# Attention stage of a GNN kernel: ACT and PE read the gathered rows in place, and a gather unit is signalled later

## What is computed

```python
h = (x @ W_att).reshape(n, H, D)
e = a_src[src] + a_dst[dst]              # per edge and head
e = jnp.where(e > 0, e, 0.2 * e)
m = jax.ops.segment_max(e, dst)          # softmax over the edges of a node
e = jnp.exp(e - m[dst]); s = jax.ops.segment_sum(e, dst)
out = jax.ops.segment_sum((e / s[dst])[:, :, None] * h[src], dst)
```

## Time and profile before

| | |
|---|---|
| median of three runs | 9094.07 us (9088.2 to 9109.1) |
| span of the profiled execution | 8395.7 us |
| first gather starts, last one ends | 3447.5 us, 5929.2 us |
| POOL, DVE, PE, ACT busy in 3447 to 5930 | 1520.6, 1935.2, 1584.9, 926.9 us |
| TensorE's granted clock there | 0.54 of full speed |
| q0 (gathers and scatters), q1 (other DMAs), share of 16 engines' span | 19.0%, 15.0% |

### The profile page before, as it was taken

The page is one execution under the profiler, slowest core; times in us unless marked ns, Lnnn a source line. Parts: engine busy times, 40 slices in busy tenths (PEclk is TensorE's granted clock), DMA queues, the critical chain, the costliest instruction groups (busy, mean ns, idle before and its releaser), DMA issues. The chain is left out here.

```text
span 8395.7 us, 119675 instructions
## 1 busy us (share of the span) xinstructions
PE 4813.9 (57%) x31076; PEld 3657.9 (44%) x31076; DVE 5547.2 (66%) x15810; ACT 3990.6 (48%) x8593; POOL 5603.9 (67%) x5190
## 2 busy tenths in 40 slices
PE   5988888888689998566666666666770000000001
PEld 3555455455378886466555555656660000000000
DVE  6999999999699997488777777878861111111111
ACT  4877777777367775333333333333332222222221
POOL 3888888888655655566666666666327777777776
PEclk9999999999789998555555555555555555555555
DMA  4444444444311112344444444444411121212121
GB/s 117 75 73 70 75 73 70 75 73 67 77 30 24 24 24 29 71 86 85 84 85 84 84 87 83 85 85 84 106 45 51 51 55 51 55 51 55 51 55 45
DMA packets 920436, 555.86 MB, mean 66 GB/s; under 512 B 811555, under 2 KB 826995, under 8 KB 910206
## 3 DMA queue, kind: packets, MB, share of 16 engines
q0 software_dynamic: 291264, 195.81, 19.0%
q1 hardware_dynamic: 626780, 352.50, 15.0%
q10 hardware_dynamic: 2304, 6.55, 0.2%
HBM read 292.89 MB, written 181.97 MB: 57 GB/s over the span
## 5 line engine op out<-in xcount | busy, mean ns | idle before, releaser
L2228 POOL DMA_INDIRECT tile_rows<-att_row_table,src_by_tile x1612 | 1520.6, 943 | 976.9 <-issue 884.0
L963 POOL DMA_INDIRECT acc<-val,idx x1116 | 1722.4, 1543 | 398.2 <-issue 318.6
L1234 POOL DMA_INDIRECT rows_l<-relation_table,idx x1612 | 1525.1, 946 | 509.2 <-issue 491.0
L736 PE MATMUL banks<-part 128*128 128x490 bf16 (+1 forms) x7440 | 1569.5, 366 | 217.8 <-DVE part L818 217.7
L1249 DVE TENSOR_TENSOR_SCAN sums_by_feature<-same_by_feature,banks 128x1728 f32<-128x1728 f32 x62 | 232.7, 3753 | 1787.8 <-ACT same_by_feature L1207 1787.8
L1276 PE MATMUL banks<-run,link 128*128 128x64 f32 x98 | 21.1, 421 | 2039.1 <-PEq L1195 2039.1
L736 PEld LDWEIGHTS banks<-part 128*128 128x128 bf16 x7440 | 694.3, 97 | 995.7 <-DVE part L818 279.9
L2321 PE MATMUL banks<-rows_l,prob 128*128 128x65 f32 x4032 | 927.7, 405 | 295.0 <-DVE kept_l L2418 269.8
L2321 PEld LDWEIGHTS banks<-rows_l,prob 128*128 128x128 f32 x4032 | 852.7, 312 | 366.2 <-DVE kept_l L2418 201.4
L1276 PEld LDWEIGHTS banks<-run,link 128*128 128x128 f32 x98 | 21.0, 333 | 2039.8 <-issue 2039.8
L894 ACT ACTIVATE digit_distance<-iota_row,dst_digits_negated 128x128 bf16<-128x128 f32 (+1 forms) x3224 | 868.8, 357 | 2.0
(11 more groups left out here) (407 smaller groups left out, 10400.8 us busy)
## 6 DMA issues: line engine op xcount, KB each, us to landing
rows_l<-tile_rows SPq DMA_DIRECT2D x2016, 38.5 KB
src_rows<-src_by_column SPq DMA_DIRECT2D x63, 1152.0 KB, 5.9
piece_sums<-kept_l SPq DMA_DIRECT2D x252, 264.0 KB
running_sums<-run SPq DMA_DIRECT2D x62, 832.0 KB, 3.6
attr<-in_edge_attr SPq DMA_DIRECT2D x61, 624.0 KB, 3.8
tile_rows<-att_row_table,src_by_tile POOLq DMA_INDIRECT x1612
rows_l<-relation_table,idx POOLq DMA_INDIRECT x1612
acc<-val,idx POOLq DMA_INDIRECT x1116
```

The lines of the kernel that those rows point to most:

```text
L736: last = e.matmul(ps[a][:, 0:ZW[a]], place0[(h * NZ + m) % 2][:, a, :], spread0[(h * NZ + m) % 2][n].rearrange("p b f -> p (b f)")[:, 0:ZW ...
L963: e.indirect_dma_start(acc_d[k], bass.IndirectOffsetOnAxis(ap=idx[h][:, r:r + 1], axis=0), val[h][:, r, :], None, compute_op=ALU.add).then ...
L1234: e.indirect_dma_start(gbuf[h][:, r, :], None, table, bass.IndirectOffsetOnAxis(ap=idx[h][:, r:r + 1], axis=0))\
L2228: e.indirect_dma_start(gathered[:, g % TRING, r, :], None, hx_d, bass.IndirectOffsetOnAxis(ap=src_col[:, t:t + 1], axis=0))\
```

## The change

SP's copies go, and with them the buffers `rows_l2_u`, their semaphores and SP's register loads. SP keeps the stores of finished units.

ACT and PE read the ring at positions held in registers. ACT loads nine values for each unit, with one load of one value (`need`) and one of eight (`place`), at the head of the turn, ahead of `tags_out`; it then waits for `s_there` itself and makes eight copies of 12 words each instead of one copy. PE loads the same eight positions at the head of the turn, ahead of `spread`, and its eight `sums` products take their moving operand at a register position. `place` and `need` now lie together, nine words for each unit.

A part of the ring is free only once PE has read it, so POOL's gate waits for `s_sum` (with an offset of SUMS0 = 2), not for `s_as`. POOL waits for the landing of gather unit g-1, and signals it, after it has issued three gathers of unit g, not ahead of all eight.

```diff
-            rows = [sb(f"rows_l2_{u}", [P, QUAD, ROW], f32, ctx) for u in range(RING)]
@@ POOL
-                            units = nc.values_load(gate[0:1, g:g + 1], [mybir.EngineType.Pool], min_val=1, max_val=NQ,
-                                                   skip_runtime_bounds_check_because=SMALL_SUM)
-                            e.wait_ge(s_as, units)
-                        if g:
-                            landed(g - 1)
+                            units = e.value_load(gate[0:1, g:g + 1], min_val=1 + SUMS0, max_val=NQ + SUMS0)
+                            e.wait_ge(s_sum, units)
+                            e.sem_inc(s_pace, 1)
                         for r in range(tiles_of(g)):
+                            if g and r == min(3, tiles_of(g) - 1):
+                                landed(g - 1)
                             t = g * QUAD + r
@@ ACT
+                    def places(i, u):
+                        j = i * RING + u
+                        at_need = place[0:1, bass.ds(j, 1), :].rearrange("n j r -> n (j r)")
+                        units = e.value_load(at_need[:, QUAD:QUAD + 1], min_val=1, max_val=TU)
+                        return loaded(at_need[:, 0:QUAD], mybir.EngineType.Activation, 0, LIMIT), units
+
+                    def logit_tags(i, u, where):
                         j = i * RING + u
-                        e.wait_ge(s_got[u], i * 16 * QUAD + 16 * QUAD)
+                        cols, units = where
+                        e.wait_ge(s_there, units)
                         e.wait_ge(s_tag, j + 1)
-                        e.copy(tags[u % 2][:, :, 0:SPLITS * HEADS], rows[u][:, :, D + 1:ROW].bitcast(bf16)).then_inc(s_as, 1)
+                        for r in range(QUAD):
+                            last = e.copy(tags[u % 2][:, r, 0:SPLITS * HEADS],
+                                          flat[:, D + 1:][:, bass.ds(cols[r], ROW - D - 1)].bitcast(bf16))
+                        last.then_inc(s_as, 1)
@@ ACT turn
+                        where = places(*at(i, u, 2)) if real(*at(i, u, 2)) else None
                         if real(i, u):
                             tags_out(i, u)
@@ PE
+                    def places(i, u):
+                        j = i * RING + u
+                        return loaded(place[0:1, bass.ds(j, 1), 0:QUAD].rearrange("n j r -> n (j r)"), mybir.EngineType.PE, 0, LIMIT)
-                                last = e.matmul(summed(r), prob[u % 2][:, r, :], rows[u][:, r, 0:W1], start=True, stop=True)
+                                last = e.matmul(summed(r), prob[u % 2][:, r, :], flat[:, bass.ds(cols[r], W1)], start=True, stop=True)
@@ PE turn
+                        cols = places(*at(i, u, -2)) if real(*at(i, u, -2)) else None
                         if real(i, u):
                             spread(i, u)
@@ SP
-                        for r in range(QUAD):
-                            e.dma_start(rows[u][:, r, :], flat[:, bass.ds(cols[r], ROW)]).then_inc(s_got[u], 16)
```

More of the change, by code:

```diff
@@ L31 @@
 TSEMS = 4
+SUMS0 = 2
 SPLITS = 3
@@ L1673, in build @@
         src_col = sb("src_by_tile", [P, TW * P], i32, maps)
-        place = sb("piece_place", [1, NQ * QUAD], i32, maps)
-        lists = own_lse[0:1, 2 * 4 * BD * HEADS:3 * 4 * BD * HEADS].bitcast(i32)
-        need, gate = lists[:, 0:KW * P // QUAD], lists[:, KW * P // QUAD:KW * P // QUAD + NG2 * P]
+        place = sb("piece_places_and_need", [1, NQ, QUAD + 1], i32, maps)
+        gate = own_lse[0:1, 2 * 4 * BD * HEADS:2 * 4 * BD * HEADS + NG2 * P].bitcast(i32)
         slot_node = sb("slot_node", [P, KW * P, 2], f32, maps)
@@ L2210, in build, with loaded @@
             SMALL_SUM = "clamped from below where it is made, and the blocks and tiles that it counts are given by the shapes"
+            flat = gathered[:, :, :, :].rearrange("p g r f -> p (g r f)")
+            LIMIT = (TRING * QUAD - 1) * ROW
+            def loaded(t, engine, low, high):
+                return nc.values_load_multi_w_load_instructions(
+                    t, [engine], min_val=low, max_val=high, skip_runtime_bounds_check_because=SMALL_SUM)[1]
             with nc.Block() as block:
@@ L2291, in _ @@
                     e.sem_inc(s_turn, 2)
-                    e.sem_inc(s_sum, RING)
+                    e.sem_inc(s_sum, SUMS0)
                     def turn_tags(i, u):
@@ L2338, in turn @@
                         if real(*at(i, u, -2)):
-                            sums(*at(i, u, -2))
+                            sums(*at(i, u, -2), cols)
                         if real(*at(i, u, -1)):
@@ L2412, in step @@
                         elif r == GROUP:
-                            e.wait_ge(s_sum, j + RING + 1)
+                            e.wait_ge(s_sum, j + SUMS0 + 1)
                             e.wait_ge(s_half, j + 3)
@@ L2456, in _ @@
                         e.sem_inc(s_kept[u], 16)
-                    flat = gathered[:, :, :, :].rearrange("p g r f -> p (g r f)")
-                    def loaded(t, at, n, low, high):
-                        return nc.values_load_multi_w_load_instructions(
-                            t[0:1, bass.ds(at, n)], [mybir.EngineType.SP], min_val=low, max_val=high,
-                            skip_runtime_bounds_check_because=SMALL_SUM)[1]
-                    def load(i, u, units):
-                        j = i * RING + u
-                        cols = loaded(place, j * QUAD, QUAD, 0, (TRING * QUAD - 1) * ROW)
-                        e.wait_ge(s_sum, j + 1)
-                        e.wait_ge(s_there, units)
-                        for r in range(QUAD):
-                            e.dma_start(rows[u][:, r, :], flat[:, bass.ds(cols[r], ROW)]).then_inc(s_got[u], 16)
-                    def store(i, u):
-                        j = i * RING + u
-                        e.wait_ge(s_run, j + 3)
-                        e.dma_start(piece_d[bass.ds(j * QUAD, QUAD), :, :].rearrange("k p f -> p k f"),
-                                    kept[u][:, :, :]).then_inc(s_kept[u], 16)
-                    def turn(i, u):
-                        if u == 0 and i is not ROUNDS:
-                            units[:] = loaded(need, i * RING + 1, RING, 1, TU)
-                        if real(*at(i, u, 1)):
-                            load(*at(i, u, 1), units[u])
-                        if real(*at(i, u, -6)):
-                            store(*at(i, u, -6))
-                    units = [None] * RING
-                    load(0, 0, loaded(need, 0, 1, 1, TU)[0])
-                    sweep(e, turn, 6)
+                    with e.Fori(0, ROUNDS) as i:
+                        for u in range(RING):
+                            j = i * RING + u
+                            e.wait_ge(s_run, j + 3)
+                            e.dma_start(piece_d[bass.ds(j * QUAD, QUAD), :, :].rearrange("k p f -> p k f"),
+                                        kept[u][:, :, :]).then_inc(s_kept[u], 16)
                     for u in range(RING):
```

20 lines of the change are left out of this document (10 added, 10 removed).

## The result

The changed kernel takes 9224.4 us (median of 4 runs, 9200.1 to 9234.7), the kernel before 9091.1 (4 runs, 9074.7 to 9109.1): a ratio of 1.0148, with a 95% interval of 1.0127 to 1.017. The forecast, 8690, had the sign wrong. Three of the four times of the kernel before are those that stand in the table ahead of the prediction.

A forecast was written before the change was run, and what follows sets the result against it. With POOL's pause closed (8.1 us a unit), DVE's 8.25 us round bounds: 251 rounds plus some 15 us end at 5560.5 instead of 5965.1, -404.6; 9094 - 405 = 8689, say 8690 us, range 8650 to 8900.

The forecast's parts named there:

- The bubble closes: POOL's 2.33 us idle between gather units falls to 0.30, with 1.7 us to spare; POOL's floor becomes about 2040 us.
- the rest of the program stays: -404.6: Code outside the gather stage keeps its time; the last L2369 starts at 5560.5 instead of 5965.1, span 7991.
- the device time is 698 us above the span, and I carry the difference to the median: Whole kernel: the 404.6 us gain on the 8395.7 us profiled span comes off the timed median, 9094 - 405 = 8689.
- Ring and gate: POOL's gate on `s_sum` and landings signalled behind the gate: no cost, 20 us if wrong by a unit now and then.
- The gate's load: POOL's single load, 0.29 us, hides in the sequencer's 5 us lead; uncovered, with check and increment, some 100 us.
- The copies: ACT's eight copies at register positions come 0.15 us apart, 0.24 at the far end, ending at 4328.1 or 4328.7.
- The loads: ACT's register loads: 0.71 us for eight, 0.29 for one, 1.35 with four short sequencer steps.
- rival (a): ACT's round becomes the bound: unaligned loads of eight cost 2.55 us, round 1.0 longer, 9.25; kernel 8940 us; chance 0.23.
- the sequencer leads by two: ACT's sequencer runs two instructions ahead, so loads start near 4327.8 and `tags_out` at 4329.2, where it was at 4327.08.
- A piece stays at 0.44: PE: each `sums` product at a register position takes 0.44 us as before, no gain or loss.
- (c): PE's products at register positions slow to 1.0 us a piece, round 11.2, kernel 9420 us, slower than before; chance 0.05.
- Wrong if L2369 waits for L2311 in most rounds: DVE's test: L2369 should start 8.2 to 8.3 us apart with no idle ahead; waiting in most rounds refutes the forecast.

The follow-up runs named there:

- A: Condition of a set of runs, not a kernel: the one in which the kernel before takes 8385 to 8389 us; its profile was taken in it.
- B: Condition of a set of runs, not a kernel: the one in which the kernel before takes 9091 to 9285 us; the times under The result are from it.
- the control: Kernel before, with POOL's gate and SP's needed-unit values loaded singly with asserted bounds, SP's store ahead of its copies: 1.0049 in A, 1.009 in B.
- Ctl5: The control run in B: 9367.4 us, 1.009 of the kernel before (9277.0).
- set 2: Runs in B of the unedited changed kernel and two variants; the kernel before takes 9285.3 us, the changed kernel 9341.1 (1.0055).
- land: The control plus only the later landing signal, after the third gather of the next unit, run in A: 7989.4 us, 0.9527 of the kernel before.
- first_land: Changed kernel with the landing signalled ahead of the gate and of the next unit's first gather, run in A: 8528.4 us, 1.0167 of the kernel before.
- again: The changed kernel unedited, run in B: 9341.1 us, 1.0055 of the kernel before.
- after_oldland: Changed kernel with the landing signalled ahead of the next unit's first gather again, behind the gate, run in B: 9116.6 us, 0.9809 of the kernel before.
- set 3: Runs in A of the unedited changed kernel and two further variants; the kernel before takes 8388.9 us, the changed kernel 8002.7 (0.954).
- ctl: The control run in A: 8424.7 us, 1.0049 of the kernel before (8384.8).
- small: Kernel of land with gathered rows of 11 words in place of 77, so sums of other data, run in A: 7989.0 us.

## Why the prediction was wrong, point by point

**POOL's part: right in A, of the wrong sign in B.** "The bubble closes" and "the rest of the program stays: -404.6" put the last L2369 at 5560.5 and the span at 7991. Measured in A: 5568.5, a span of 8003.5, and the first round at 3476.4 for 3474.7; the time falls by 386 us (8388.9 to 8002.7). In B the table gives the two halves of the change: closing the pause costs 230 us with ring reads (2915 against 2685) and 375 with SP's copies; ring reads in place of the copies bring 258 with the pause and 403 without. Together they bring 2943 - 2915 = 28 us against the control. Ctl5 is 90 us above the kernel before; if all of that lies in this stage, an estimate, the kernel before has some 2853 there and the change costs 62, near the +56 us of set 2. The first comparison has +133, and why it is larger is open; the changed kernel's stage there is 3638.0 to 6503.8, 2866 us.

**The step that failed** is this one: "the device time is 698 us above the span, and I carry the difference to the median". No 698 us lie outside the span, though the section on the profile of before says so too. In every later run the time is 1.7 to 1.8 us above the span (9234.71 and 9233.0 for the changed kernel). The timed runs of before were made in B, its profiled one in A. So a gain read from an A profile was taken off a B time, where the change costs 133 us (56 in set 2). I had seen the gap and given it no rival. Behind it stands a term that the sum took at nothing, the way from the end of PE's work to its signal. That is right in the profile it was read from (0 of 1204 late); in B 496 of 1051 signals come late, by up to 34 us, and closing the pause costs 230 us of stage in place of gaining 405.

The Trainium skill ("Runtime: NRT & Kernel Launch", "The ~15µs preamble/postamble breakdown") has a gap of some 6 us between a profile's total and the reported time, the same for every kernel, with the profile the longer. The runs here show the reported time 1.7 to 1.8 us above the span, the other way round; neither leaves room for 698.

**Ring and gate, "costed at nothing, 20 us if wrong":** in A 53.9 us of POOL's idle time ends at the gate, and the last round is 9 us behind land's (5568.5 and 5559.5), the slower loads included. In B the same gate has 721 and 773 us.

**The gate's load, "without that cover some 100 us":** 108 us in first_land, where the cover is gone, with a part that can be the gate's own wait. In the changed kernel POOL's whole idle time in A is 38 us above land's (552.6 and 514.7), and the waits at the gate sum to more than that.

**ACT.** The copies stand 0.11 apart (0.15 taken). The loads were mis-sized: 1.75 us for the eight in place of 0.71, 0.77 for the single one (the L2248 load's median) in place of 0.29. That is rival (a)'s mechanism, taken at 0.32 a value and measured at 0.22, and on PE at 0.29. Its price, 1.0 us a round, didn't come: 8.335 against 8.283. By (a)'s numbers `tags_out` starts 4.2 us after the first copy; it starts 4311.06 - 4307.98 = 3.08 after it. The copies and loads are shorter than (a) had them, and the loads begin earlier: "the sequencer leads by two" was wrong. The load of one value starts at 4308.0, with the first of the eight copies, so the sequencer had all eight copies issued ahead of it; over the 251 rounds the load starts a median 0.04 us after the first copy. The queue of eight, which the prediction quoted and set aside, fits this; the one step at 4326.7 was too little to read the lead from.

The Trainium skill ("Runtime: NRT & Kernel Launch", "Instruction fetch mechanics") has 200 ns a register, for loads from HBM; the lists here lie in SBUF. It is near the nine-word lists (0.22 and 0.29) and off for the aligned ones (0.11 on ACT, 0.07 on PE).

**PE.** "A piece stays at 0.44": it does (four in A in 4308.70 - 4306.94 = 1.76 us, starts of the second half and of `turn_exps`), and the mean of one product's matmul is 411 ns in A and 417 in B, so (c) falls in both conditions. What made the kernel slower was none of the mechanisms listed: it was the signal after the product, not the product.

**"Wrong if L2369 waits for L2311 in most rounds":** the wait came, not in most rounds. In 63 of 252 DVE waits for "remote", 711 us in all, which is `spread` with a signal that had not arrived.

## What to carry to other kernels

Compare the span of the profiled execution with the timed runs before anything is summed: a gap of some per cent means that the profile shows another condition than the times, and each mechanism needs a second price for it. A pause that looks like pure loss can keep other engines' holds short: in B the signals came out behind a row of gathers, and closing the pause cost 2.5% (again against after_oldland); where a releaser in the profile is a DMA of another stage or "remote", look at the semaphore's own event beside the end of the work that raises it. Of the orders measured here, ring reads with the landing signalled early are the best in B (0.981), not to be told from the changed kernel with the long memset (0.983); in A the changed kernel or the late landing alone are (0.954, 0.953). None was measured better than the kernel before in both, but neither of the two that gain in B was run in A. The changed kernel with the long memset is one to try in A: with the shorter ones it took 0.954 and 0.964 there.

## What the runs showed of the hardware

- Two conditions, 8.4 to 10.7% apart for the kernel before, 15 to 17% for the changed one (8003 against 9224 and 9341 us), 22% for the late landing alone (7989 and 9775). One chip showed B in set 2 and A in set 3; what sets the condition is open.
- In B, PE's semaphore signals are held in the stage of the gathers, most of them until a row of gathers is over; ACT's and DVE's never are. They keep their order: in the six B traces no PE signal overtakes an earlier one, and held ones come out in bursts, often 0.09 us apart. The gathered data isn't held: the last packet of a gather moves 1.2 us after the gather's end (medians by its place in the row 1.2 to 2.4) in both conditions, also for the sixteenth in a row. Whether the bytes, the descriptors or the signals of the gathers are the load is open, since small never met B.
- In B, the 1612 gathers of L1235 keep the pitch of 1.25 us for the first 185 or so; from there the mean pitch is 1.40. It isn't an even slowing: more than half still come 1.25 us apart, and about 100 come 2.0 apart. In A they stay at 1.25.
- In B most events of the gathers' own semaphores are missing from the trace: 3898 of 25792 recorded in the changed kernel, 25018 in ctl in A. It may have the same cause as the late signals; no run tests that. Nor does any run tell whether the recording is itself part of the load: every timed run of the experiments has a recorded span.
- A load of eight registers takes 0.59 us on PE and 0.89 on ACT from a list at multiples of eight words, 2.35 and 1.75 from one at multiples of nine; among the latter, those that start at a multiple of four words take 1.00 and 0.55. Matmuls at register positions cost what static ones do, 0.44 us a piece.
